# Moving the turn of the expert rows by one chunk, and other VectorE work between a chunk's inputs and its weights

## Chip, cores and metric

The kernel runs on one core of one Trainium2 chip. The metric is the device time of one execution in microseconds (us). The time of the kernel before is the median of three runs.

## What is computed

Four sequences of 1024 tokens with 128 features pass through four blocks, each followed by a residual sum and a layer norm: a state-space mixer with a gated MLP (L0 attention), a mixture of 8 linear experts with the best 2 per token (L0 ffn), an attention of 16 heads with relative positions (L1 attention), and a second mixture of 8 gated experts with a capacity of 512 rows (L1 ffn).

```python
x = _layernorm(x + _L0_attn_ref(x, ...))   # mixer, then MLP
x = _layernorm(x + _L0_ffn_ref(x, ...))    # 8 experts, best 2
x = _layernorm(x + _L1_attn_ref(x, ...))
x = _layernorm(x + _L1_ffn_ref(x, ...))
```

In the first expert layer each token's logits give a softmax, the two largest shares are kept, and the output is the sum of the two experts' products weighted by these shares.

## The kernel before, in words

Every engine has its own written-out program; engines meet at semaphores only, and each engine takes its instructions in order. The first phase, up to about 560 us, runs the first two blocks and the projections of the attention. Then comes the attention (560 to about 1270 us), then the second expert layer.

The first phase is a pipeline over the four sequences, written as a table of slots:

```python
SLOTS = [(0, None, None), (1, 0, None), (2, 1, 0), (3, 2, 1), (None, 3, 2), (None, None, 3)]
SCALED_AT = {3: (0,), 4: (1, 2), 5: (3,), 6: (4, 5), 7: (6,)}
BIAS_AT, LAST_PAIR = 5, 7
```

In a slot (m, p, q), sequence m is in the mixer, p in the MLP and the first expert layer, q in the projections to queries, keys and values. Slots are counted from 0 here, so slots 1, 2 and 3 hold a mixer and an expert layer together, slots 2, 3 and 4 an expert layer and projections.

The second half of a slot is a loop of eight turns c = 0 to 7, one for each chunk of 128 tokens of the mixer's scan; the parts of p and q are spread over the same turns. For the mixer, turn c has these steps:

- **TensorE**: `chunk_carried` (the carried state's output), `chunk_state` (the new state), then for chunk c + 1 `chunk_front` (three transposes and one product) and `chunk_after` (sums of decays), then `chunk_out` (the output of chunk c).
- **ScalarE**: `chunk_copy` (line 1347, which waits for VectorE's `Gm`) and `chunk_exp` (line 1353, the decays L) of chunk c + 1, then `decays_so_far` (line 1364, four copies) of chunk c + 2.
- **GpSimd**: `chunk_decays`, two products of 128x256: `xw` (line 1613), which needs VectorE's inputs, and `hdec` (line 1617), which `chunk_carry` of the next turn needs.
- **VectorE**: `chunk_carry` (line 1973, needs the new state from TensorE and `hdec`), `chunk_scaled` (1990), then for chunk c + 1 `chunk_inputs` (1964, and 1967, which writes `Gm`) and `chunk_weights` (1979, needs `Gm` and ScalarE's L).

Into the same turns go the steps of the expert layer of p: VectorE's `normalise` (line 1866, eight instructions, in turn 0) writes the rows `x2`; TensorE's `rows_turned_moe` transposes them; ScalarE's `evac_T("moe", ...)` (1238) copies the result to `xnT`; TensorE's `route0` forms the routing logits; VectorE's `route_logits` and `route_shift` (1878 to 1885) take them in turn 1, ScalarE's `route_exp` and VectorE's `route_shares` (from 1889) follow in turn 2, and `route_which` to `gate_parts` in turn 3. TensorE's `expert_pair` k = 0 to 7 multiplies two tiles of rows with four experts; VectorE's `experts_scaled(p, k)` (2084) adds the products with their shares, 8 instructions for each k, by the table `SCALED_AT`. In turn 5 `bias_added` (2065) follows.

For q, queries and keys are cut into three bf16 parts: ScalarE's `cut_part` (1322, 1324, in turns 0, 1 and 2) writes a part, and VectorE's `cut_rest` (2129, 2133, in turns 0 and 1) subtracts it. `cut_part` s = 1 and 2 need the remainder of s - 1.

## Time and profile before

| what | us |
|---|---|
| median of 3 runs (1388.61 to 1392.61) | 1392.61 |
| the profiled execution, its own time | 1390.74 |
| its span, first to last instruction | 1389.0 |
| VectorE busy in the span | 1090.6 (79%) |
| TensorE matmuls busy in the span | 1239.2 (89%) |

All views read one execution. Times in them are from the start of the span. A bracket at a row's end says how long the engine was idle before it and what released it. Instructions of an engine overlap a little, so a start can lie before the end of the row ahead.

The slots lie about so: slot 1 from 112 to 190 us, slot 2 to 312, slot 3 to 438, slot 4 to 526, slot 5 to 560.

### The profile page before, as it was taken

The numbers are of one execution on the slowest core, as the hardware profiler recorded it, in microseconds if no ns is written. First come the engines' busy times: TensorE is split into PE (matmuls) and PEld (weight loads), VectorE is DVE, ScalarE is ACT, GpSimd is POOL, SyncE is SP. The second block draws the span as 40 slices with busy tenths as digits, with TensorE's granted clock in tenths as the row PEclk, the third lists the DMA queues.
The fourth block names the chain that finished last, engine by engine and source line by source line (L and its number), as shares of the span: only waits on it lengthen the run. The fifth ranks groups of instructions, "written<-read, shape, count | busy, mean of one in ns | idle before, by whom it ended". The sixth has DMA issues, their size and how long they took to land. (4 is left out here: it accounts for less than half of the span.)

```text
span 1389.0 us, 39431 instructions
## 1 busy us (share of the span) xinstructions
PE 1239.2 (89%) x16528; PEld 647.8 (47%) x16528; DVE 1090.6 (79%) x2184; ACT 902.1 (65%) x1739; POOL 285.0 (21%) x417
## 2 busy tenths in 40 slices
PE   5998888788887877999999999999999999994895
PEld 2556445453644522454555444444444544432462
DVE  6787787789676688899999989999999998944123
ACT  5665345437432302899998888888889988893242
POOL 2222131121112104200000110511104211034472
PEclk9999999999989988999999999999999999997998
DMA  5080000200113812111102211122102200011135
GB/s 141 1 230 16 1 2 16 108 2 1 61 49 74 152 68 109 44 38 44 43 17 62 52 45 35 46 68 54 43 18 56 62 22 18 18 34 46 45 108 188
DMA packets 59703, 77.72 MB, mean 56 GB/s; under 512 B 15010, under 2 KB 41189, under 8 KB 57686
## 3 DMA queue, kind: packets, MB, share of 16 engines
q1 hardware_dynamic: 56454, 70.95, 19.2%
q0 software_dynamic: 3072, 4.25, 1.0%
q8 instruction: 131, 2.15, 0.7%
q14 instruction: 46, 0.38, 0.1%
HBM read 37.18 MB, written 40.03 MB: 56 GB/s over the span
## 5 line engine op out<-in xcount | busy, mean ns | idle before, releaser
L1479 ACT ACTIVATE space<-ps 128x512 f32<-128x512 f32 x1024 | 605.2, 598 | 86.4 <-PE ps L667 37.2
L2139 DVE TENSOR_REDUCE smax<-ps 128x1 f32<-128x1024 f32 x512 | 613.3, 1220 | 51.1 <-PE ps L667 26.4
L667 PE MATMUL ps<-space 96*32 96x512 bf16 (+2 forms) x8432 | 609.9, 381 | 24.8 <-DVE smax L2139 13.8
L667 PEld LDWEIGHTS ps<-space 96*32 96x32 bf16 (+2 forms) x8432 | 251.4, 98 | 292.1 <-DVE smax L2139 44.2
L1047 PE MATMUL ps<-space 128*9 128x256 f32 x4096 | 315.8, 379 | 0.0
L1047 PEld LDWEIGHTS ps<-space 128*9 128x9 f32 x4096 | 116.2, 92 | 100.1 <-ACT space L1479 0.4
L1347 ACT ACTIVATE btok<-ps 128x128 f32<-128x128 f32 x32 | 8.9, 277 | 125.5 <-issue 101.5
L667 PE MATMUL ps<-w_exp,xnT 128*128 128x512 f32 x128 | 72.4, 694 | 14.4 <-DVE x L2084 14.4
L2084 DVE SCALAR_TENSOR_TENSOR x<-ps,gsel,x 128x128 f32<-128x128 f32 x256 | 69.1, 342 | 12.4 <-PE ps L667 12.1
L667 PE MATMUL ps<-ones,ident 128*128 128x512 bf16 x228 | 58.8, 418 | 17.4 <-POOLq L1695 12.3
L1949 DVE SCALAR_TENSOR_TENSOR space<-space,conv_w 128x512 f32<-128x512 f32 x96 | 71.2, 750 | 2.3
L1584 POOL TENSOR_SCALAR eps_sum<-mv 128x4 f32<-128x4 f32 x32 | 7.4, 231 | 318.3 <-DVEq L1855 317.6
L1691 POOL DMA_INDIRECT expert_in<-space,slot x64 | 63.0, 984 | 34.9 <-issue 19.3
L667 PE MATMUL ps<-space,w_in 128*128 128x512 f32 x96 | 58.6, 719 | 8.2 <-DVE x L2019 3.3
L1675 POOL TENSOR_TENSOR xnT<-x,xa 128x512 f32<-128x512 f32 x6 | 7.7, 1282 | 233.4 <-DMA xa<-den_rows 233.4
L1613 POOL TENSOR_TENSOR space<-space,decay 128x256 f32<-128x256 f32 x28 | 17.1, 612 | 155.6 <-issue 109.8
L667 PEld LDWEIGHTS ps<-ones,ident 128*128 128x128 bf16 x228 | 23.6, 106 | 50.4 <-issue 18.2
L1979 DVE TENSOR_TENSOR space<-space,Gm 128x512 f32<-128x512 f32 x32 | 24.6, 769 | 27.2 <-ACT space L1353 27.2
L667 PEld LDWEIGHTS ps<-w_exp,xnT 128*128 128x128 f32 x128 | 25.3, 215 | 44.0 <-issue 23.7
L1586 POOL TENSOR_TENSOR rstd<-eps_sum,neg_half 128x4 f32<-128x4 f32 x40 | 41.6, 1039 | 3.3
L1364 ACT ACTIVATE aU<-upto,av 128x128 f32<-128x128 f32 x128 | 40.6, 395 | 0.0
L667 PE MATMUL ps<-xnT,w_gate 128*128 128x512 f32 x64 | 34.9, 628 | 5.6 <-DVE space L2038 4.8
(250 smaller groups left out, 1375.4 us busy)
## 6 DMA issues: line engine op xcount, KB each, us to landing
head_sums<-space SPq DMA_DIRECT2D x31, 256.0 KB, 2.3
q_rows<-space SPq DMA_DIRECT2D x24, 256.0 KB, 2.4
k_rows<-space SPq DMA_DIRECT2D x24, 256.0 KB, 2.8
space<-k_rows SPq DMA_DIRECT2D x16, 384.0 KB, 5.4
space<-q_rows SPq DMA_DIRECT2D x16, 384.0 KB, 7.1
expert_out<-x_all SPq DMA_DIRECT2D x2, 2048.0 KB, 18.5
space<-expert_out SPq DMA_DIRECT2D x4, 1024.0 KB, 9.5
v_rows<-space SPq DMA_DIRECT2D x4, 576.0 KB, 3.3
```

Of the source, the lines that this page charges most:

```text
L667: return nc.tensor.matmul(out, lhsT, rhs, start=first, stop=last)
L1047: last = nc.tensor.matmul(bank(run_bank(N))[COLS * g:COLS * g + VSTEP, q0:q0 + PV_COLS], v_now[:, b % 2, kt, lo:lo + VSTEP], prob[:, QUAD ...
L1347: nc.scalar.activation(btok[:, c % 2], bank(TRB)[:, 2 * P:3 * P], ACT.Copy).then_inc(S.btok_ready, 1)
L1364: last = nc.scalar.activation(aU[:, c % 2, h], upto[:], ACT.Copy, scale=av[:, c, h:h + 1])
L1479: nc.scalar.activation(prob[:, QUAD * (step % PROB_SETS) + unit % QUAD, :], bank(STB + unit % 2), ACT.Exp)\
L1586: g.tensor_tensor(out, eps_sum[:, 0:n], neg_half[:, 0:n], ALU.pow).then_inc(done, 1)
L1613: g.tensor_tensor(xw[:, c % 2], xdt[:, c % 2], decay[:, 0, c].unsqueeze(2).to_broadcast([P, SSM_HEADS, SSM_DIM]), ALU.mult).then_inc(S.xw_ ...
L1691: g.indirect_dma_start(expert_in, bass.IndirectOffsetOnAxis(ap=slot[:, k, i:i + 1], axis=0), xrow[:, i, k, :], None, bounds_check=E * CAPA ...
L1949: ins = v.scalar_tensor_tensor(out, raw[:, f, lo + k:lo + k + HALF], conv_w[:, f, k:k + 1], out, ALU.mult, ALU.add)
L1979: v.tensor_tensor(Wm[:, c % 2], EL[:, c % 2], Gm[:, c % 2].unsqueeze(1).to_broadcast([P, SSM_HEADS, P]), ALU.mult).then_inc(S.w_ready, 1)
L2084: ins = v.scalar_tensor_tensor(x2[:, i, :], tiles4(EXPERT_BANKS[k][w])[:, e, :], gsel[:, i, HT * (k % 2) + e:HT * (k % 2) + e + 1], x2[:, ...
L2139: v.tensor_reduce(smax[:, N % 2, i:i + 1], ps[:, b0:b0 + 2, :].rearrange("p k n -> p (k n)"), AX.X, ALU.max).then_inc(S.s_max, 1)
```

## The change

Nothing is computed differently, only the order of instructions on TensorE, ScalarE and VectorE changes; GpSimd's and SyncE's programs stay.

- `rows_turned_moe` moves from the end of turn 0 to turn 1, after `chunk_after` and ahead of `chunk_out`; `evac_T("moe", ...)` moves to turn 1 too, behind that turn's copy, exponential and decays, and so behind `cut_part` of turn 0.
- On VectorE `normalise` moves ahead of `chunk_weights` in turn 0.
- `cut_rest` s = 0 and 1 move from the end of turns 0 and 1 to turns 1 and 2, ahead of `chunk_weights`.
- In turns 4 and 6 the first of the two `experts_scaled` (k = 1 and k = 4) moves ahead of `chunk_weights`.

```diff
--- before.py
+++ after.py
@@ -960,6 +960,8 @@
                             chunk_state(m, c)
                             chunk_front(m, c + 1)
                             chunk_after(m, c + 1)
+                    if p is not None and c == 1:
+                        rows_turned_moe(p)
                     if p is not None and c == BIAS_AT:
                         gates_turned(p)
                     if p is not None and c in PRODUCTS_AHEAD:
@@ -973,8 +975,6 @@
                         if c == NT - 1:
                             mix_out(m, 0)
                     if p is not None:
-                        if c == 0:
-                            rows_turned_moe(p)
                         if c == 1:
                             route0(p)
                         if c == 2 and m is None:
@@ -1426,7 +1426,7 @@
                         evac_gates(p)
                     if m is not None and c in (2, 4, 6):
                         gated_squares(m, c // 2 - 1)
-                    if p is not None and c == 0:
+                    if p is not None and c == 1:
                         evac_T("moe", p, (7, 5))
                     if p is not None and c == 2:
                         route_exp(p)
@@ -2191,6 +2191,19 @@
                         chunk_carry(m, c)
                         chunk_scaled(m, c)
                         chunk_inputs(m, c + 1)
+                    if p is not None and c == 0:
+                        for H in range(2):
+                            normalise(xa, x2, H, 0, 6 * p + H)
+                    if q is not None and p is not None and c in (1, 2):
+                        cut_rest(q, c - 1)
+                    if m is not None and p is not None and HT <= c < NT - 1:
+                        ahead = SCALED_AT[c][:1]
+                    else:
+                        ahead = ()
+                    for k in ahead:
+                        if c != BIAS_AT:
+                            experts_scaled(p, k)
+                    if m is not None and c < NT - 1:
                         chunk_weights(m, c + 1)
                     if m is not None and c == NT - 1:
                         chunk_scaled(m, c)
@@ -2201,9 +2214,6 @@
                         if m + 1 < B:
                             input_norm(m + 1)
                     if p is not None:
-                        if c == 0:
-                            for H in range(2):
-                                normalise(xa, x2, H, 0, 6 * p + H)
                         if c == 1:
                             route_logits(p, 6, b_route0)
                             route_shift(p)
@@ -2216,15 +2226,14 @@
                             gate_parts(p)
                     if p is not None:
                         for k in SCALED_AT.get(c, ()):
-                            experts_scaled(p, k)
+                            if k not in ahead or c == BIAS_AT:
+                                experts_scaled(p, k)
                             if c == BIAS_AT:
                                 bias_added(p)
                                 expert_statistics(p, 0)
                             if m is None and k in MAXIMA_IN_SUMS:
                                 for pair in MAXIMA_IN_SUMS[k]:
                                     pair_max(pair)
-                    if q is not None and p is not None and c < 2:
-                        cut_rest(q, c)
                     if m is not None and c % 2 == 1 and c < NT - 1:
                         gate(m, c // 2)
                 if m is not None:
```

VectorE, slot 2, turns 0 and 1, in the kernel before (1973 carry, 1990 scaled, 1964 and 1967 inputs, 1979 weights, 1866 normalise, 2129 and 2133 remainders):

```order
L1964 TENSOR_TENSOR space<-ps,dt 128x256
L1967 TENSOR_TENSOR Gm<-ps,upto 128x128
L1979 TENSOR_TENSOR space<-space,Gm 128x512
L1866 TENSOR_SCALAR x<-xa,mv,rstd 128x128 x8
L2129 TENSOR_TENSOR space<-space 128x1024
L2133 TENSOR_TENSOR space<-space 128x1024
L1973 TENSOR_TENSOR hst<-hdec,ps 128x256
L1990 TENSOR_TENSOR space<-ps,decay 128x256
L1964 TENSOR_TENSOR space<-ps,dt 128x256
L1967 TENSOR_TENSOR Gm<-ps,upto 128x128
```

and with the change:

```order
L1964 TENSOR_TENSOR space<-ps,dt 128x256
L1967 TENSOR_TENSOR Gm<-ps,upto 128x128
L1866 TENSOR_SCALAR x<-xa,mv,rstd 128x128 x8
L1979 TENSOR_TENSOR space<-space,Gm 128x512
L1973 TENSOR_TENSOR hst<-hdec,ps 128x256
L1990 TENSOR_TENSOR space<-ps,decay 128x256
L1964 TENSOR_TENSOR space<-ps,dt 128x256
L1967 TENSOR_TENSOR Gm<-ps,upto 128x128
L2129 TENSOR_TENSOR space<-space 128x1024
L2133 TENSOR_TENSOR space<-space 128x1024
L1979 TENSOR_TENSOR space<-space,Gm 128x512
```

Each of the two weights now has other work between it and its inputs, and the remainders stand one turn later, behind the second inputs.

ScalarE, slot 2, turns 0 and 1 (1238 copies the turned rows to `xnT`, 1322 and 1324 cut queries and keys, 1347 to 1364 are the copy, the exponential and the decays):

```order
-L1238 ACTIVATE xnT<-ps 128x512 x2
-L1322 ACTIVATE space<-space 128x1024
-L1324 ACTIVATE space<-space 128x1024
-L1347 ACTIVATE btok<-ps 128x128
-L1353 ACTIVATE space<-ps 128x512
-L1364 ACTIVATE aU<-upto,av 128x128 x4
+L1322 ACTIVATE space<-space 128x1024
+L1324 ACTIVATE space<-space 128x1024
+L1347 ACTIVATE btok<-ps 128x128
+L1353 ACTIVATE space<-ps 128x512
+L1364 ACTIVATE aU<-upto,av 128x128 x4
+L1238 ACTIVATE xnT<-ps 128x512 x2
```

The copy of the turned rows went from ahead of the first cut to behind the next chunk's decays.

VectorE, slot 2, turn 4 (2084 adds the scaled expert products):

```order
 L1964 TENSOR_TENSOR space<-ps,dt 128x256
 L1967 TENSOR_TENSOR Gm<-ps,upto 128x128
-L1979 TENSOR_TENSOR space<-space,Gm 128x512
-L2084 SCALAR_TENSOR_TENSOR x<-ps,gsel,x 128x128 x16
+L2084 SCALAR_TENSOR_TENSOR x<-ps,gsel,x 128x128 x8
+L1979 TENSOR_TENSOR space<-space,Gm 128x512
+L2084 SCALAR_TENSOR_TENSOR x<-ps,gsel,x 128x128 x8
 L1973 TENSOR_TENSOR hst<-hdec,ps 128x256
```

Eight of the sixteen instructions went ahead of the weights.

## Rows read from the trace of the kernel before

**Rows 1.** Busy time by engine, slot 2 (us: PE, PEld, DVE, ACT, POOL; clock, DMA, GB/s)

```profile
190.00:312.00 122.00, 102.07 (x742) 60.51 (x746) 96.37 (x292) 59.25 (x144) 23.71 (x37) 0.93 0.10 36
```

**Rows 2.** Waits of VectorE from 120 to 440 us: total us, times, longest us

```profile
DVE space L1979 <- ACT space L1353: 20.2, 22, 1.7
...
DVE space L2129 <- ACT space L1322: 6.2, 4, 2.6
...
DVE red L1889 <- ACT sc L1334: 3.1, 3, 1.0
```

**Rows 3.** Timeline of VectorE, slot 2: start us, us, instructions, [idle before <-releaser]

```profile
245.68 0.80 DVE L1979 TENSOR_TENSOR space<-space,Gm 128x512 f32<-128x512 f32 x1 [0.88 <-ACT space L1353]
246.40 2.13 DVE L1866 TENSOR_SCALAR x<-xa,mv,rstd 128x128 f32<-128x128 f32 x8
251.15 1.23 DVE L2129 TENSOR_TENSOR space<-space 128x1024 f32<-128x1024 f32 x1 [2.62 <-ACT space L1322]
...
254.42 0.28 DVE L1967 TENSOR_TENSOR Gm<-ps,upto 128x128 f32<-128x128 f32 x1
...
268.01 0.42 DVE L1973 TENSOR_TENSOR hst<-hdec,ps 128x256 f32<-128x256 f32 x1 [1.16 <-PE ps L667]
```

**Rows 4.** Timeline of ScalarE, slot 2

```profile
249.57 0.60 ACT L1238 ACTIVATE xnT<-ps 128x512 f32<-128x512 f32 x1 [0.65 <-PE ps L654]
...
255.43 1.27 ACT L1364 ACTIVATE aU<-upto,av 128x128 f32<-128x128 f32 x4
```

**Rows 5.** Timeline of TensorE, slot 2: the routing products

```profile
255.55 0.72 PE L667 MATMUL ps<-w_route,xnT 128*32 128x8 f32 x64
```

**Rows 6.** Timeline of VectorE, slot 1

```profile
125.74 0.69 DVE L1979 TENSOR_TENSOR space<-space,Gm 128x512 f32<-128x512 f32 x1 [1.69 <-ACT space L1353]
...
130.17 0.42 DVE L1973 TENSOR_TENSOR hst<-hdec,ps 128x256 f32<-128x256 f32 x1 [1.68 <-PE ps L667]
...
133.41 0.23 DVE L1878 TENSOR_TENSOR lg<-ps,b_route 128x64 f32<-128x64 f32 x1 [0.29 <-PE ps L667]
```

**Rows 7.** Timeline of TensorE, slot 1: last products of loop turn 0

```profile
126.02 0.71 PE L769 MATMUL ps<-ident,space 128*128 128x128 f32 x4
```

**Rows 8.** Timeline of VectorE, slot 3

```profile
390.20 0.42 DVE L1973 TENSOR_TENSOR hst<-hdec,ps 128x256 f32<-128x256 f32 x1 [1.22 <-PE ps L667]
```

**Rows 9.** Timeline of VectorE, slot 4

```profile
481.61 1.22 DVE L2129 TENSOR_TENSOR space<-space 128x1024 f32<-128x1024 f32 x1 [2.32 <-ACT space L1322]
...
498.36 2.16 DVE L2084 SCALAR_TENSOR_TENSOR x<-ps,gsel,x 128x128 f32<-128x128 f32 x8 [1.14 <-PE ps L667]
```

**Rows 10.** Timeline of TensorE, slot 4

```profile
494.07 0.62 PE L667 MATMUL ps<-space 96*32 96x512 bf16 x8 [2.51 <-DVE smax L2139]
```

**Rows 11.** Timeline of VectorE, slot 2, loop turn 4

```profile
279.11 0.78 DVE L1979 TENSOR_TENSOR space<-space,Gm 128x512 f32<-128x512 f32 x1 [0.88 <-ACT space L1353]
```

**Rows 12.** Timeline of VectorE, slot 1: weights beside GpSimd

```profile
121.35 0.91 DVE L1979 TENSOR_TENSOR space<-space,Gm 128x512 f32<-128x512 f32 x1 [0.88 <-ACT space L1353]
```

**Rows 13.** Timeline of GpSimd, slot 1: its carry product at that place

```profile
121.67 1.06 POOL L1617 TENSOR_TENSOR hdec<-hst,decay 128x256 f32<-128x256 f32 x1
```

**Rows 14.** All weights and all carry products: duration ns min/median/max, first and last start

```profile
L1979 DVE TENSOR_TENSOR space<-space,Gm x32: 681/785/910, 43.0 to 420.3; 128x512 f32<-128x512 f32 x32
...
L1617 POOL TENSOR_TENSOR hdec<-hst,decay x28: 612/612/1062, 42.6 to 408.1; 128x256 f32<-128x256 f32 x28
```

**Rows 15.** Busy time and granted clock of a short stretch (columns as in Rows 1)

```profile
157.00:161.00 4.00, 3.76 (x6) 1.22 (x6) 2.16 (x6) 2.54 (x11) 1.18 (x2) 0.50 0.00 0
```

**Rows 16.** Timeline of TensorE, slot 1, loop turn 5: one expert pair

```profile
157.24 3.78 PE L667 MATMUL ps<-w_exp,xnT 128*128 128x512 f32 x4 [1.83 <-DVE x L2084]
```

**Rows 17.** Timeline of TensorE, slot 2, loop turn 4: one expert pair

```profile
275.59 1.98 PE L667 MATMUL ps<-w_exp,xnT 128*128 128x512 f32 x4 [1.08 <-DVE x L2084]
```

**Rows 18.** Timeline of VectorE, slot 1, loop turn 5

```profile
161.13 2.16 DVE L2084 SCALAR_TENSOR_TENSOR x<-ps,gsel,x 128x128 f32<-128x128 f32 x8 [1.09 <-PE ps L667]
164.53 1.48 DVE L2065 TENSOR_TENSOR x<-x,ps 128x512 f32<-128x512 f32 x2 [1.24 <-PE ps L667]
```

## The prediction

> **What bounds the kernel now.** I read the busy times by stretch first, then the list of waits, then the timelines of the slots that the change touches. In slot 2 VectorE is busy 96.37 of 122 us and TensorE's matmuls, whose spans overlap, 102.07 [rows 1]: neither is full, so it is waits that matter, and which of them lie on a chain. VectorE's list has three that the change aims at: 20.2 us in 22 waits of the weights for ScalarE's exponential, 6.2 us in 4 waits of the remainders for ScalarE's cut, 3.1 us in 3 waits of the routing shares [rows 2]. They are on the path that ends last, because the others mostly wait for VectorE's last result, as the brackets on TensorE show (a maximum, a scaled sum) [rows 10, 16, 17]. So a wait that VectorE loses moves everything behind it, up to the next point where VectorE waits for something that does not move. The attention behind the first phase starts when the last slot's work is done, and keeps its length.
>
> The regular wait is 0.88 us [rows 3, 11]: VectorE has written `Gm`, ScalarE then copies and exponentiates, and only then can the weights run. Work put there, as long as it is over 0.88 us and ready, removes it. Nothing is added or removed; the same instructions run.
>
> **Slot 2.** In turns 0, 1 and 2 the fillers are 2.13 us of normalise [rows 3] and twice two remainders of 1.23 us [rows 3]; each is over 0.88, so 3 x 0.88 = 2.64 goes. The remainders waited 2.62 [rows 3] and, in the next turn, about 0.6 (the four waits of slots 2 and 3 sum to 6.2 [rows 2]; with 2.62 here, and 2.32 for the long one of slot 3 as in slot 4 [rows 9], 1.2 is left for the two short ones): ScalarE's first cut stood behind the copy of the turned rows, which stood behind normalise, transposes and all. Now the cut runs while VectorE normalises, and is there before it is asked for: 3.2 goes. The shares waited 1.03, a third of 3.1 [rows 2], so the exponential they need ends 0.88 + 0.79 + 1.03 = 2.7 us behind `Gm`, and now 2.3 of remainders and 0.7 of weights lie between: it goes. The carry of turn 3 waited 1.16 for TensorE [rows 3]; TensorE's expert pair ahead of it starts when `chunk_scaled` is done, and 2.3 us more of VectorE's work now lies between that and the carry: it goes. Sum removed: 2.64 + 3.2 + 1.03 + 1.16 = 8.0.
>
> What is late next is the turned rows. Call T the end of the second `Gm` (254.42 + 0.28 in the old order). ScalarE's decays end 2.0 us behind it, at 256.70 [rows 4]; now the two copies of 0.60 [rows 4] follow, overlapping a little, to T + 3.1, and the routing product of 0.72 [rows 5] to T + 3.8. VectorE has the remainders and weights, 2.3 + 0.7, ready at T + 3.0, so `route_logits` waits 0.8 that it did not wait before. Behind it in order stand the gate and the next carry. Net of turns 0 to 2: 8.0 - 0.8 = 7.2.
>
> In turns 4 and 6 the filler is eight scaled sums, 2.16 us [rows 9], whose products TensorE forms a turn earlier (turn 4) or in the same turn ahead of the chunk's output (turn 6; if they come late, at worst the 0.88 comes back). 2 x 0.88 = 1.8 [rows 11].
>
> **A new cost: GpSimd beside VectorE.** GpSimd starts its two products of 0.61 us as soon as the inputs are written, so they ran in the gap that is now filled. Where one met VectorE's weights, both stretched: the weights took 0.91 [rows 12] and the carry product 1.06 [rows 13], against minima of 0.68 and 0.61 [rows 14]; usually the weights take 0.79, the tail of a GpSimd product costing 0.1. The scaled sums read PSUM and one tensor of SBUF; no row shows them beside GpSimd, and I take none for them. For a filler of turns 0 to 2 the bounds are 0 (0.1 less than now, as the weights no longer meet GpSimd) and 1.22 (both products ahead of VectorE); I take 0.45, the stretch of 1.06 - 0.61, as the nearest row. In slots 2 and 3 it counts in turns 0 and 2, since in turn 1 the 0.8 wait takes it up: 0.9 for each.
>
> The Trainium skill (SBUF — State Buffer, SBUF: two separate sides) has a rule against this change: VectorE and GpSimd share one pair of ports, and whichever of a VectorE instruction with two SBUF inputs or in a two-port mode and a GpSimd instruction that reads SBUF starts first holds it for its whole length. The stretched pair [rows 12, 13] agrees. By that rule GpSimd, which starts first, would hold each filler back for up to both products, and the sum would be that of the second rival below.
>
> Slot 2: 7.2 + 1.8 - 0.9 = 8.1.
>
> **Slot 3** is the same, with 1.22 [rows 8] for the carry's 1.16: the remainders lose 3.0 (6.2 less 3.2), so 2.64 + 3.0 + 1.03 + 1.22 = 7.9 goes, 0.8 comes, + 1.8 - 0.9: 8.0.
>
> **Slot 1** has no q, so no remainders. `Gm` of turn 0 ended at 125.74 - 1.69 = 124.05 [rows 6]. Normalise and weights now end at 124.05 + 2.13 + 0.69 = 126.9. The carry waited until 130.17 [rows 6], because TensorE put the transposes ahead of the state product. Without them TensorE is free at 126.7 [rows 7] and has two products of 256 columns to do, at most 1.0 by half of an expert pair [rows 17]: carry at 127.8 (bounds 126.9 and 130.17), 2.4 earlier. T, four instructions of 0.3 to 0.4 later, is 129.05. But with no remainders VectorE is idle from weights to T + 3.8 = 132.85, against 133.41 before [rows 6]: of 2.4 only 0.5 is kept, the rest turns into a wait of about 2.2 at `route_logits`. With 1.8 from turns 4 and 6: 2.3. GpSimd's stretch disappears in the wait for the state.
>
> **Slot 4** has no mixer; only ScalarE's order changes. The remainders' wait of 2.32 [rows 9] goes but for 0.1: 2.2. TensorE's idle 2.51 in front of a score pair [rows 10] shrinks by as much, and the wait of 1.14 for the next expert pair [rows 9], which then ran slow, goes: 3.3 (bounds 0 and 5.6, the latter if a later pair gains the 2.33 that rows 18 show).
>
> **Sum**: 2.3 + 8.1 + 8.0 + 3.3 = 21.7. From the profiled execution's own 1390.74: **1369.0**. That execution lies 1.9 under the median of the runs shown, 1392.61, so the same gain from the median would be 1370.9.
>
> **Rivals.**
>
> *TensorE keeps its clock.* In turn 5 of slots 1 and 3 an expert pair takes 3.78 [rows 16] at a granted clock of 0.50, the 1.2 GHz level [rows 15], against 1.98 in slot 2 [rows 17], behind 1.83 us of idle; VectorE then waits 1.09 + 1.24 = 2.33 [rows 18]. With eight sums done ahead of the weights, what TensorE waits for there comes earlier, and its idle time is shorter. If both stay fast: 2 x 2.33 more, 1364.3. Against: no row shows which idle time decides. Chance 0.13.
>
> *GpSimd holds VectorE for both products.* 1.22 instead of 0.45 in turns 0 and 2, and 0.4 over the 0.8 in turn 1, in slots 2 and 3: 2 x (2 x 0.77 + 0.4) = 3.9, 1372.9. For it: GpSimd is first by the timeline, and its results are not late. Against: the only rows show 0.1 to 0.45. Chance 0.16.
>
> *The routing chain is longer.* If TensorE runs turn 1 at the low level, the outputs and routing products ahead of `route_logits` double, up to 2 more in slots 1 to 3: about 1375. The change shortens TensorE's idle time there, which speaks against it. Chance 0.07.
>
> *Slower.* The place is TensorE's clock over the loops: every expert pair at the low level costs VectorE what turn 5 shows, 2.33. The 32 pairs of slots 1 to 4 would have to hold 11 slow ones more than now to eat 21.7 and 4.2 besides (26 / 2.33); with 12, 1369.0 + 28 = 1397. It would take longer idle stretches on TensorE, and the change shortens them. Chance 0.02.
>
> *Nothing moves*, because something that VectorE does not drive, such as the loads for the attention, sets the end of the first phase: 1391. The profile shows no such wait. Chance 0.03.
>
> **How the numbers follow.** The forecast has 0.59, with the rivals 0.13, 0.16, 0.07, 0.02 and 0.03. The range takes in the first two rivals (1364 to 1373) with some 2 to 4 us on each side for slot 4's bounds and for the spread of runs, 1388.61 to 1392.61: **1361 to 1377**. About 0.3%, 4.2 us, is what a measurement of this kernel can tell: faster 0.95, same 0.03, slower 0.02.
>
> **What would show it.** In the new profile the weights' waits for the exponential should fall from 22 to about 9 between the same slots (turns 3 and 5 of three slots, turns 1 and 2 of slot 1, little else); the remainders should not wait; `route_logits` should wait about 2.2 in slot 1 and up to 0.8 in slots 2 and 3; the shares and the carry of turn 3 should not wait in slots 2 and 3. GpSimd's products or the fillers should be longer by some tenths. The attention should begin about 22 us earlier and last as long. It would be wrong if `route_logits` waited over 3 us, or if the expert pairs at the low clock became more.

## The result, and the profile after

| | before | after |
|---|---|---|
| median of the timed runs, us | 1390.61 (4 runs) | 1365.79 (4 runs, 1364.55 to 1367.16) |
| the profiled execution's span, us | 1389.0 | 1362.8 |
| VectorE busy in the span, us | 1090.6 | 1091.7 |
| TensorE's matmuls busy in the span, us | 1239.2 | 1225.2 |
| GpSimd busy in the span, us | 285.0 | 295.2 |
| start of the attention in the profile, us | 559.67 | 533.55 |

The ratio of the times is 0.9833, with a 95% interval of 0.9811 to 0.9855: 20.2 to 26.3 us faster, 24.8 between the medians. The forecast was 1369.0, a gain of 21.7. VectorE does the same work in the same busy time; waits went. GpSimd is busy 10 us more: its products were held up beside VectorE's work, as will be seen.

Slot 2, in the columns of [rows 1]: it is 8.1 us shorter with VectorE busy for the same time.

```profile
184.30:298.20 113.90, 99.18 (x748) 59.38 (x752) 96.82 (x291) 59.06 (x144) 28.59 (x37) 0.94 0.11 39
```

VectorE's waits in the new profile from 118 to 425 us, the same slots as in [rows 2] (columns: total us, times, longest us).

```profile
DVE space L1979 <- ACT space L1353: 7.9, 9, 0.9
...
DVE lg L1878 <- PE ps L667: 4.5, 3, 2.1
...
DVE red L1889 <- ACT sc L1334: 1.0, 1, 1.0
```

The weights wait 9 times instead of 22, as forecast; the remainders (L2129) no longer stand in the list; the shares (L1889) wait in one slot only. New is the wait of the logits (L1878), 2.14 us in slot 1, 1.28 and 1.11 in slots 2 and 3.

VectorE's timeline of the new profile, slot 2, turns 0 to 2, against [rows 3].

```profile
238.98 2.84 DVE L1866 TENSOR_SCALAR x<-xa,mv,rstd 128x128 f32<-128x128 f32 x8
...
243.34 0.28 DVE L1967 TENSOR_TENSOR Gm<-ps,upto 128x128 f32<-128x128 f32 x1
243.54 1.21 DVE L2129 TENSOR_TENSOR space<-space 128x1024 f32<-128x1024 f32 x1
...
245.81 0.68 DVE L1979 TENSOR_TENSOR space<-space,Gm 128x512 f32<-128x512 f32 x1
247.77 0.23 DVE L1878 TENSOR_TENSOR lg<-ps,b_route 128x64 f32<-128x64 f32 x1 [1.28 <-PE ps L667]
...
251.17 1.22 DVE L2129 TENSOR_TENSOR space<-space 128x1024 f32<-128x1024 f32 x1
252.30 1.63 DVE L2133 TENSOR_TENSOR space<-space 128x1024 f32<-128x1024 f32 x1
253.86 1.10 DVE L1979 TENSOR_TENSOR space<-space,Gm 128x512 f32<-128x512 f32 x1
...
256.29 0.42 DVE L1973 TENSOR_TENSOR hst<-hdec,ps 128x256 f32<-128x256 f32 x1
```

The carry of turn 3 (the last row) has no bracket. Between its second `Gm` and that carry the kernel before took 268.01 - 244.52 = 23.5 us, the change 256.29 - 238.79 = 17.5: 6.0 less, against 7.2 - 0.9 = 6.3 forecast.

GpSimd's timeline of the new profile, slot 2, turns 0 to 2: L1613 is the product for the state, L1617 the one for the carry.

```profile
239.01 0.61 POOL L1613 TENSOR_TENSOR space<-space,decay 128x256 f32<-128x256 f32 x1 [6.96 <-DVE space L1964]
239.59 0.62 POOL L1617 TENSOR_TENSOR hdec<-hst,decay 128x256 f32<-128x256 f32 x1
243.55 3.41 POOL L1613 TENSOR_TENSOR space<-space,decay 128x256 f32<-128x256 f32 x1 [3.35 <-issue]
...
251.19 1.67 POOL L1613 TENSOR_TENSOR space<-space,decay 128x256 f32<-128x256 f32 x1 [3.65 <-issue]
252.82 1.59 POOL L1617 TENSOR_TENSOR hdec<-hst,decay 128x256 f32<-128x256 f32 x1
```

Three places, three outcomes, though by the trace VectorE's work starts first in each, by 0.01 to 0.03 us. In turn 0 GpSimd is undisturbed and normalise takes 2.84 instead of 2.13: 0.71 lost. The loss lies in the first two of its eight instructions, which end 0.08 us behind GpSimd's second product; shown alone they are this row of VectorE's timeline:

```profile
238.98 1.30 DVE L1866 TENSOR_SCALAR x<-xa,mv,rstd 128x128 f32<-128x128 f32 x2
```

In turn 1 VectorE is undisturbed and GpSimd's product takes 3.41 instead of 0.61. In turn 2 both pay: second remainder 1.63 for 1.22, weights 1.10 for 0.68, so 0.83 lost. There the engines take turns, one whole instruction each: first remainder, product, second remainder, product and weights end at 252.39, 252.86, 253.93, 254.41 and 254.96. In turn 4 the scaled sums and GpSimd's products run side by side, and neither is longer than alone (VectorE's timeline, then GpSimd's):

```profile
266.43 2.15 DVE L2084 SCALAR_TENSOR_TENSOR x<-ps,gsel,x 128x128 f32<-128x128 f32 x8
```

```profile
266.45 0.61 POOL L1613 TENSOR_TENSOR space<-space,decay 128x256 f32<-128x256 f32 x1 [7.76 <-issue]
```

TensorE's timeline of the new profile, slot 2, turn 1; then the busy times and the granted clock (0.50) of the two us from the routing products on, in the columns of [rows 1]; then ScalarE's copies of the turned rows. After the transposes (L654) and the output of the chunk TensorE is idle 1.96 us until ScalarE has copied, and then the routing products and those of the state run slow.

```profile
242.43 1.04 PE L654 MATMUL ps<-ident,x 128*128 128x128 f32 x8
...
246.65 1.04 PE L667 MATMUL ps<-w_route,xnT 128*32 128x8 f32 x64 [1.96 <-ACT xnT L1238]
247.63 1.22 PE L667 MATMUL ps<-hst,space 128*128 128x256 f32 x2
```

```profile
246.60:248.60 2.00, 1.95 (x66) 1.79 (x67) 0.77 (x4) 1.89 (x3) 0.93 (x2) 0.50 0.34 122
```

```profile
245.52 1.08 ACT L1238 ACTIVATE xnT<-ps 128x512 f32<-128x512 f32 x2
```

TensorE's expert pair of turn 5, slot 1, in the new profile, and VectorE's sums and bias that waited for it in [rows 18]: the pair takes 1.99 us, not the 3.78 of [rows 16], and both waits are gone.

```profile
154.93 1.99 PE L667 MATMUL ps<-w_exp,xnT 128*128 128x512 f32 x4 [1.49 <-DVE x L2084]
```

```profile
157.65 2.15 DVE L2084 SCALAR_TENSOR_TENSOR x<-ps,gsel,x 128x128 f32<-128x128 f32 x8
159.84 1.28 DVE L2065 TENSOR_TENSOR x<-x,ps 128x512 f32<-128x512 f32 x2
```

The time from profile to profile, slot by slot, in us. A slot is read here from VectorE's second `Gm` in it to the start of the last four sums of the mixer's residual (line 2019 of the kernel before); "1 to 2" and "2 to 3" are the stretches between; "slot 4" runs from the end of slot 3 to the start of the attention on TensorE. The last column is the ratio of the timed runs to those of the kernel before, with its interval. The experiments follow below.

| profile | slot 1 | 1 to 2 | slot 2 | 2 to 3 | slot 3 | slot 4 | attention starts | ratio |
|---|---|---|---|---|---|---|---|---|
| before | 66.49 | 54.26 | 69.49 | 52.94 | 71.19 | 121.53 | 559.67 | 1 |
| before, again | 66.48 | 53.89 | 68.17 | 52.96 | 69.74 | 120.02 | 554.83 | 1.0016 [0.9997, 1.0034] |
| the change | 60.87 | 54.27 | 61.38 | 54.32 | 60.89 | 118.17 | 533.55 | 0.9833 [0.9811, 0.9855] |
| the change, again | 61.30 | 52.89 | 61.33 | 54.34 | 60.80 | 118.59 | 533.53 | 0.9836 [0.9815, 0.9857] |
| scalings only | 61.56 | 52.88 | 67.32 | 54.28 | 65.50 | 121.28 | 546.67 | 0.9932 [0.9911, 0.9954] |
| no scalings | 63.13 | 52.89 | 63.16 | 52.94 | 62.52 | 115.77 | 535.29 | 0.9873 [0.9849, 0.9898] |
| fast clock | 63.67 | 54.25 | 69.27 | 54.32 | 70.03 | 119.06 | 554.90 | 0.9967 [0.9955, 0.9979] |
| no turn | 60.09 | 52.88 | 62.00 | 54.33 | 61.48 | 117.71 | 532.74 | 0.9848 [0.9826, 0.9870] |
| slot 4 old | 60.93 | 53.41 | 61.03 | 52.96 | 60.87 | 121.74 | 535.16 | 0.9837 [0.9810, 0.9864] |
| small products | 59.80 | 52.88 | 59.33 | 52.95 | 58.68 | 117.42 | 524.13 | 0.9769 [0.9743, 0.9795] |
| gate first | 60.13 | 52.89 | 61.19 | 54.32 | 60.83 | 118.26 | 532.22 | 0.9809 [0.9782, 0.9836] |
| searches first | 60.15 | 52.89 | 60.22 | 52.94 | 59.85 | 118.68 | 528.92 | 0.9789 [0.9766, 0.9813] |
| copies first | 60.83 | 52.88 | 60.01 | 52.95 | 59.46 | 115.75 | 525.71 | 0.9802 [0.9780, 0.9823] |
| copies and searches first | 58.16 | 52.89 | 58.95 | 54.32 | 58.34 | 116.78 | 523.08 | 0.9776 [0.9755, 0.9797] |

What lies behind the start of the attention takes 828.1 to 832.9 us in these profiles, with no order that follows the edits, so the columns of the slots tell more than the span.

### The profile page after: what moved, and what is told of

The parts are those of the page before. It is cut to its first block and busy times, and to the rows that moved or that the text cites. A ratio compares the mean times of both kernels' runs of the same rounds, so it can differ in the third digit from the quotient of the medians.

```text
span 1362.8 us, 39431 instructions
## 1 busy us (share of the span) xinstructions
PE 1225.2 (90%) x16528; PEld 644.6 (47%) x16528; DVE 1091.7 (80%) x2184; ACT 901.7 (66%) x1739; POOL 295.2 (22%) x417
## 5 line engine op out<-in xcount | busy, mean ns | idle before, releaser
L667 PE MATMUL ps<-w_exp,xnT 128*128 128x512 f32 x128 | 66.4, 643 | 12.8 <-DVE x L2084 12.8
L1613 POOL TENSOR_TENSOR space<-space,decay 128x256 f32<-128x256 f32 x28 | 24.9, 889 | 129.6 <-issue 83.7
```

Of the source, the lines that this page charges most:

```text
L667: return nc.tensor.matmul(out, lhsT, rhs, start=first, stop=last)
L1613: g.tensor_tensor(xw[:, c % 2], xdt[:, c % 2], decay[:, 0, c].unsqueeze(2).to_broadcast([P, SSM_HEADS, SSM_DIM]), ALU.mult).then_inc(S.xw_ ...
```

## The experiments

**How much is chance.** The change and the kernel before were each run and profiled once more.

> The change once more, unaltered, to tell what of the differences between the experiments belongs to the kernel and what to the execution. Where TensorE fell to the low level in the profile of the change (the hidden layer's products in the first halves of slots 2 and 3, 1.4 us each against other experiments) it falls again if the program's own timing decides it: the stretches between the slots are 54.3 and 54.3 us again, and the attention starts within 1 us of 533.55. If chance in the execution decides, these stretches differ by 1.4 from one profile to the next.

> The kernel before once more, unaltered. If its own timing makes TensorE fall to the low level in turn 5 of slots 1 and 3, as in its first profile, the expert pair takes 3.78 us there again (from the sixth to the seventh Gm of the slot 11.8 us instead of 9.3), in slot 2 1.98. If it was chance in that one execution, at least one of the two is fast now or slot 2 is slow, and the 4.8 us that the change gained there are not the change's.

The start of the attention repeats within 0.02 us for the change, but only because differences cancel: the stretch "1 to 2" is 52.89 instead of 54.27, while slot 1 is 0.4 longer and began 0.6 later. "2 to 3" repeats at 54.34. In "1 to 2" TensorE's products for the MLP's hidden layer were slow in the first profile of the change (granted clock 0.57 from 215.6 to 217.4 us) and not in the second (1.00 from 216.6 to 217.8), behind a little less idle time (TensorE's timeline, first the change, then the change again):

```profile
215.60 1.88 PE L667 MATMUL ps<-xnT,w_gate 128*128 128x512 f32 x2 [2.04 <-DVE space L2038]
```

```profile
216.67 1.12 PE L667 MATMUL ps<-xnT,w_gate 128*128 128x512 f32 x2 [1.71 <-DVE space L2038]
```

So a piece of 1.4 us can come or go from one execution to the next. The kernel before, profiled again, starts its attention 4.8 us earlier than the first time, in pieces of 1.3 to 1.5 in slots 2, 3 and 4. The slow pairs of turn 5 are there again in slots 1 and 3, a little shorter, and in slot 2 not:

```profile
158.01 3.30 PE L667 MATMUL ps<-w_exp,xnT 128*128 128x512 f32 x4 [1.83 <-DVE x L2084]
...
404.55 3.54 PE L667 MATMUL ps<-w_exp,xnT 128*128 128x512 f32 x4 [1.83 <-DVE x L2084]
```

From the seventh to the eighth `Gm` of the slot (number 6 and 7, counted from 0; turn 5 lies between) it takes 10.6 and 10.5 us there, 11.8 in both slots the first time, 9.3 in slot 2, where the pair is fast: these waits belong to the kernel, their length varies.

Slot 2's piece of 1.3 is, but for 0.2, the wait of 1.16 of the carry of turn 3 [rows 3], which the prediction counted among the waits that the order of the instructions makes. TensorE's expert pair ahead of that carry took 2.63 us in the first profile of the kernel before and 1.88 in the second, and there the carry doesn't wait (TensorE's timelines, first and second profile):

```profile
264.38 2.63 PE L667 MATMUL ps<-w_exp,xnT 128*128 128x512 f32 x4
```

```profile
262.73 1.88 PE L667 MATMUL ps<-w_exp,xnT 128*128 128x512 f32 x4
```

The granted clock was 0.64 in the first (262.3 to 267.0 us), 1.00 in the second (261.6 to 264.7). Over slots 2 and 3 of the four profiles that keep VectorE's old order in turns 0 to 3 (the kernel before twice, "scalings only" and "fast clock") the carry waits 1.16 to 1.24 in the six where this pair ran slow and not in the two where it ran fast. So this wait was the clock's, too.

**The sums ahead of the weights, and TensorE's clock in turn 5.** First the sums alone, in the kernel before:

```diff
+                        if p is not None and c in (4, 6):
+                            experts_scaled(p, SCALED_AT[c][0])
                         chunk_weights(m, c + 1)
...
```

> The kernel before with one part of the change alone: in turns 4 and 6 of slots 1 to 3 eight of the scaled sums stand ahead of the weights. Both theories give a gain of 1.19 (turn 4) and 0.92 (turn 6) per slot, as the change showed: 3 x 2.1 = 6.3 us. Theory A: the sums done earlier also shorten TensorE's idle time ahead of turn 5's expert pair and so keep its clock in slots 1 and 3; then that pair takes 1.98 instead of 3.78 us, the waits of 1.09 + 1.24 for it go, and the gain is 6.3 + 2 x 2.4 = 11.1 us, a ratio to the kernel before of 0.992. Theory B: the clock in turn 5 came from what the change moved in turns 0 to 3; then the pair stays at 3.78 in slots 1 and 3, the gain is 6.3, the ratio 0.9955.

Then the change without them:

```diff
-                    if m is not None and p is not None and HT <= c < NT - 1:
-                        ahead = SCALED_AT[c][:1]
-                    else:
-                        ahead = ()
+                    ahead = ()
```

> The change without the sums ahead of the weights in turns 4 and 6; the rest of it stays. Theory A (the sums ahead keep TensorE's clock in turn 5): the pair of turn 5 in slots 1 and 3 takes 3.78 again and VectorE waits 1.09 + 1.24 for it, so 11.1 of the 26 us gained are lost, ratio about 0.991. Theory B (what was moved in turns 0 to 3 keeps it): the pair stays at 1.98, 6.3 are lost, ratio about 0.988.

The pair of turn 5 in slot 1, with the sums alone and with the rest alone (TensorE's timelines):

```profile
155.62 1.99 PE L667 MATMUL ps<-w_exp,xnT 128*128 128x512 f32 x4 [1.49 <-DVE x L2084]
```

```profile
157.33 1.98 PE L667 MATMUL ps<-w_exp,xnT 128*128 128x512 f32 x4 [1.83 <-DVE x L2084]
```

Alone, the sums shorten slots 1 to 3 by 4.9, 2.2 and 5.7 us, in slots 1 and 3 with a fast pair: theory A's 11.1 and some more, of which 1.2 lies between the fourth and fifth `Gm` of slot 3, where the edit does nothing (the carry's wait above, which did not occur there this time). Taking them out of the change costs 2.3, 1.8 and 1.6 in the slots, 5.7 in all, and the pairs stay fast: theory B's figure. So either half of the change is enough to free turn 5 of the low clock, and theory A's second prediction fell. The idle time right ahead of the pair does not decide it: it is 1.83 where the pair is slow [rows 16] and 1.83 in the row above. Whether it takes part was asked by filling it, in the kernel before:

```diff
                     if p is not None and c == BIAS_AT:
                         gates_turned(p)
+                        if m is not None:
+                            keep_clock(4, 6)
```

> The kernel before, and on TensorE six products of the identity with ones, written to a bank that nobody reads, between the turned gates and the expert pair of turn 5 in slots 1 to 3: they fill part of its 1.83 us of idle time there and change nothing else. If that idle time lowers the clock, the pairs of slots 1 and 3 take 1.98 instead of 3.78 and VectorE's waits of 1.09 + 1.24 go in both: 4.7 us less, ratio 0.9966; the idle time left is about 0.5. If the clock falls for another reason, the pairs stay at 3.78, the six products themselves run longer, and the time is the same or up to 1 us longer per slot.

TensorE's timeline, slot 1, turn 5, of that kernel:

```profile
155.45 1.46 PE L667 MATMUL ps<-ones,ident 128*128 128x512 bf16 x6
157.44 1.98 PE L667 MATMUL ps<-w_exp,xnT 128*128 128x512 f32 x4 [0.53 <-DVE x L2086]
```

The pair is fast in both slots, turn 5 takes 9.26 us in both, and the timed runs gain 0.0033 [0.0021, 0.0045], 4.6 us, against 4.7 expected. By the timed runs the low clock in turn 5 cost 2.9 to 6.2 us, which fits the waits of the first profile; this profile alone would not show it, since its attention starts where that of the kernel before, again, does (554.90 and 554.83). What else, ahead of that idle time, has to come together is open.

**The turn of the rows.** TensorE and ScalarE at their old places, VectorE as in the change:

```diff
-                    if p is not None and c == 1:
-                        rows_turned_moe(p)
...
+                        if c == 0:
+                            rows_turned_moe(p)
...
-                    if p is not None and c == 1:
+                    if p is not None and c == (1 if m is None else 0):
                         evac_T("moe", p, (7, 5))
```

> The change with the turn of the rows put back to turn 0 on TensorE and on ScalarE in slots 1 to 3 (slot 4 keeps the new order); VectorE's order is that of the change. Theory 1, the prediction's: the turn one chunk later is worth little by itself, since what it takes from the carry comes back as the wait of the routing logits (2.1 us in slot 1, 1.1 to 1.3 in slots 2 and 3). Then the wait of the logits vanishes, the carry of turn 1 waits 1 to 3 us for TensorE instead, and the time is within 2 us of the change: ratio 0.982 to 0.985. Theory 2: the turn's place is a main term; then the carry's wait (up to 3 us in slot 1) and late cuts on ScalarE (the remainders wait about 1 us again) come on top, 5 us or more slower than the change, ratio 0.987 or higher.

VectorE's timeline, slot 2: the carry of turn 1, and the logits behind the weights.

```profile
241.93 0.42 DVE L1973 TENSOR_TENSOR hst<-hdec,ps 128x256 f32<-128x256 f32 x1 [1.08 <-PE ps L667]
...
246.84 0.21 DVE L1878 TENSOR_TENSOR lg<-ps,b_route 128x64 f32<-128x64 f32 x1
```

The slots are 0.8 shorter, 0.6 longer and 0.6 longer than in the change: 0.4 in sum, and the ratio is 0.9848, at the end of theory 1's range. Theory 1 holds: one wait (1.1 us for the state) is traded for another (1.3 for the logits). In slots 1 to 3 the gain is VectorE's order; the turn on TensorE and ScalarE is worth next to nothing there. One thing more is traded: with the old place GpSimd's product of turn 1 is not starved, it gets in behind the first remainder as in turn 2, and the second remainder pays, in slots 2 and 3 alike (slot 2, turn 1, VectorE's and GpSimd's timelines):

```profile
244.26 1.64 DVE L2133 TENSOR_TENSOR space<-space 128x1024 f32<-128x1024 f32 x1
```

```profile
243.15 1.67 POOL L1613 TENSOR_TENSOR space<-space,decay 128x256 f32<-128x256 f32 x1 [4.52 <-issue]
```

**Slot 4.** ScalarE's old order there alone:

```diff
-                    if p is not None and c == 1:
+                    if p is not None and c == (0 if m is None else 1):
                         evac_T("moe", p, (7, 5))
```

> The change with ScalarE's old order in slot 4 alone: there the turned rows are copied ahead of the first cut again. The prediction's term for slot 4 says that the attention starts 3.3 us later behind the start of slot 4 than in the change (the first remainder waits 2.3 us again, and the expert pair 1.1), ratio to the kernel before 0.9857 instead of 0.9833. The rival, that slot 4's gain came from the phase at which the slot is reached: the attention starts within 1 us of the change.

VectorE's timeline, slot 4, with the old order:

```profile
457.02 1.23 DVE L2129 TENSOR_TENSOR space<-space 128x1024 f32<-128x1024 f32 x1 [2.32 <-ACT space L1322]
...
473.82 2.16 DVE L2084 SCALAR_TENSOR_TENSOR x<-ps,gsel,x 128x128 f32<-128x128 f32 x8 [1.19 <-PE ps L667]
```

Both waits of [rows 9] are back, and slot 4 takes 121.74 instead of 118.17 and 118.59: 3.2 to 3.6 longer, as the prediction's term has it. Over all profiles of the table slot 4 takes 119.1 to 121.7, mean 120.7, in the five with the old order, 115.8 to 118.7, mean 117.5, in the nine with the new. The ratio does not show it: 0.9837 against the change's 0.9833 where 0.9857 was expected, and its interval holds all three. In the profile the two stretches between the slots were 2.2 shorter that time, so the attention starts only 1.6 later.

**GpSimd beside VectorE.** Its two products cut to one column in 64 (this kernel leaves out most of the carried state in slots 1 to 3):

```diff
-                g.tensor_tensor(xw[:, c % 2], xdt[:, c % 2],
+                n = SSM_DIM if b == 0 else 1
+                g.tensor_tensor(xw[:, c % 2, :, 0:n], xdt[:, c % 2, :, 0:n],
...
-                g.tensor_tensor(hdec[:], hst[:, c % 2],
+                g.tensor_tensor(hdec[:, :, 0:n], hst[:, c % 2, :, 0:n],
...
```

> The change with GpSimd's two products of a chunk cut to one column of 64 per head in slots 1 to 3 (the carried state is then not what the reference has, so the routing and what hangs on it differ; the start of the attention is what is read). If GpSimd's reads stretch VectorE's fillers: normalise of turn 0 takes 2.13 instead of 2.84, the second remainder of turn 2 1.22 instead of 1.63, the weights behind it 0.69 instead of 1.10, and the attention starts 2 x 1.5 + 0.7 = 3.7 us earlier than in the change at most, 2 at least (part is taken up by waits for the turned rows). If they are long for another reason (ScalarE, their own data), their durations stay and the start moves by less than 1 us.

VectorE's normalise (turn 0) and second remainder (turn 2) of that kernel, slot 2, then GpSimd's products of turns 0 and 1:

```profile
235.95 2.14 DVE L1867 TENSOR_SCALAR x<-xa,mv,rstd 128x128 f32<-128x128 f32 x8
...
248.23 1.22 DVE L2134 TENSOR_TENSOR space<-space 128x1024 f32<-128x1024 f32 x1
```

```profile
235.98 0.20 POOL L1614 TENSOR_TENSOR space<-space,decay 128x4 f32<-128x4 f32 x1 [7.80 <-DVE space L1965]
...
239.82 2.99 POOL L1614 TENSOR_TENSOR space<-space,decay 128x4 f32<-128x4 f32 x1 [3.47 <-issue]
```

VectorE's durations are back, so the stretch came from GpSimd's products. The slots are 1.1, 2.1 and 2.2 us shorter, 5.3 in sum where 3.7 was expected at most: the logits waited 0.94 for 1.28, too, and the weights took 0.69 for 0.78 in the turns that still wait. (The other 4.1 of the earlier attention lie between the slots, in slot 4 and ahead of slot 1, in pieces that vary between other profiles too.) The last row is the clearest reading of the study: a product of four columns, 0.20 us of work, takes 2.99, and ends at 242.81, as VectorE's two remainders and the weights behind them end (242.75).

The Trainium skill (SBUF — State Buffer, SBUF: two separate sides) calls the pair of ports shared by the two engines an exclusive lock, not a split of bandwidth. The traces agree that one side stands still while the other runs: GpSimd in turn 1, each in its turn in turn 2, the first two instructions of normalise in turn 0. In two points they don't bear out what the prediction drew from the rule. By the starts in the trace VectorE comes first in all three turns, and yet normalise is the side that waits in turn 0; and it lost 0.71, not 1.22.

**Three further steps.** The gate ahead of the logits in turn 1:

```diff
                         if c == 1:
+                            if m is not None:
+                                gate(m, 0)
                             route_logits(p, 6, b_route0)
...
```

> The change, and in turn 1 of slots 1 to 3 the gate of the first two chunks (three instructions, 1.5 us) stands on VectorE ahead of the routing logits instead of behind them. It needs only the outputs of chunks 0 and 1, which TensorE has some 0.7 us before the routing product. If the wait of the logits (2.1, 1.3, 1.1 us) is on the path, 0.7 to 1.5 of it goes in each slot: the attention starts about 3 us earlier than in the change, ratio to the kernel before 0.981. If the wait hid something else (ScalarE's exponential for the shares, TensorE's next chunk), it comes back behind and the start moves by less than 1 us.

VectorE's timeline, slot 2: the logits no longer wait, the carry behind them does.

```profile
246.83 0.21 DVE L1878 TENSOR_TENSOR lg<-ps,b_route 128x64 f32<-128x64 f32 x1
...
248.62 0.42 DVE L1973 TENSOR_TENSOR hst<-hdec,ps 128x256 f32<-128x256 f32 x1 [1.07 <-PE ps L667]
```

Slots 2 and 3 gain 0.2 and 0.1, slot 1 0.7, and the attention starts 1.3 earlier, not 3. The ratio, 0.9809, is the expected 0.981, but its interval holds the change's 0.9833, and the slots don't show the gain. A miss, near to what the rival said: TensorE forms the routing products ahead of the state, so what delays the one delays the other. What delays both is ScalarE's copy. It was put ahead of the next chunk's copy and exponential:

```diff
+                    if p is not None and m is not None and c == 1:
+                        evac_T("moe", p, (7, 5))
                     if m is not None and c < NT - 1:
                         chunk_copy(m, c + 1)
                         chunk_exp(m, c + 1)
...
-                    if p is not None and c == 1:
+                    if p is not None and m is None and c == 1:
                         evac_T("moe", p, (7, 5))
```

> The change with one step of ScalarE put earlier: in turn 1 of slots 1 to 3 it copies the turned rows ahead of the next chunk's copy and exponential instead of behind the chunk's decays. Theory: what delays the routing product, the logits, and behind them on TensorE the state product of the next carry is ScalarE's place for the copies (they wait for nothing else: the transposes end before the second Gm of the turn). Then the routing product starts about 2 us earlier, at full clock since TensorE's idle 1.96 us ahead of it is gone, the logits wait for under 0.3 us in slots 2 and 3, and the next carry comes 1.3 us earlier in slots 2 and 3 and 1.7 in slot 1 (there the weights start 0.5 later): the attention starts 4.4 us earlier. Rival: GpSimd's product for the state, starved beside the remainders until 246.9, holds the next carry where it is in slots 2 and 3; then the carry waits for it, and only slot 1's 1.7 is gained.

TensorE's timeline, slot 2, turn 1:

```profile
243.38 0.72 PE L667 MATMUL ps<-w_route,xnT 128*32 128x8 f32 x64
...
245.77 0.70 PE L667 MATMUL ps<-space,btok 128*128 128x256 f32 x2 [1.03 <-POOL space L1615]
```

The logits wait for nothing, and the next `Gm`, number 3, stands 1.36 and 1.32 us closer behind number 1 in slots 2 and 3, as expected. TensorE now waits for GpSimd's starved product, but ends in time for the carry. In slot 1 it was 0.5 where 1.7 was expected, and as much is lost again at the slot's end, in VectorE's waits for TensorE. With no remainders ahead of them, VectorE's weights wait for the exponential that now stands behind the copy (VectorE's timeline, slot 1):

```profile
131.34 0.69 DVE L1981 TENSOR_TENSOR space<-space,Gm 128x512 f32<-128x512 f32 x1 [2.33 <-ACT space L1353]
```

Most of these 2.33 us are not the order's. TensorE ran turn 0 of this slot at a granted clock of 0.58 (123.0 to 126.7 us) and turned the rows at 128.87; in the run with both steps, below, the same products ran at 1.00, the rows were turned at 127.09, and the weights waited 1.09 (TensorE's timelines, this run and that one):

```profile
123.09 1.92 PE L667 MATMUL ps<-aU,after 128*128 128x512 f32 x2
```

```profile
122.72 1.02 PE L667 MATMUL ps<-aU,after 128*128 128x512 f32 x2
```

The attention starts 7.8 us earlier, but only 2.8 of it in slots 1 to 3; slot 4 (2.4) and the stretches between (2.8) are nothing that the edit touches. The third step is the searches of the routing ahead of the weights in turn 3:

```diff
+                    if m is not None and p is not None and c == HT - 1:
+                        route_which(range(NT))
                     for k in ahead:
...
                         if c == HT - 1:
-                            route_which(range(NT))
+                            if m is None:
+                                route_which(range(NT))
```

> The change, and in turn 3 of slots 1 to 3 the eight index searches of the routing (1.15 us) stand on VectorE between the chunk's inputs and its weights, where it still waits 0.9 us for the exponential. By the mechanism that the prediction used, the three waits go, less what GpSimd's two products cost beside the searches: 1.5 to 2.6 us, ratio to the kernel before about 0.982. If VectorE is not what bounds turn 3, the time saved turns up as a wait at the next carry, and the start of the attention moves by less than 0.5 us.

VectorE's weights and GpSimd's products beside the searches, slot 2, turn 3:

```profile
257.07 0.69 DVE L1979 TENSOR_TENSOR space<-space,Gm 128x512 f32<-128x512 f32 x1
```

```profile
255.88 0.61 POOL L1613 TENSOR_TENSOR space<-space,decay 128x256 f32<-128x256 f32 x1 [3.11 <-issue]
256.45 0.61 POOL L1617 TENSOR_TENSOR hdec<-hst,decay 128x256 f32<-128x256 f32 x1
```

The wait is gone, neither engine is stretched, and from `Gm` number 4 to number 5 each slot is 1.06 us shorter, 0.88 of it the wait and 0.1 the weights, which no longer meet GpSimd. Slots 1 to 3 together gain 2.9, a little more than the 2.6 expected.

> The step of evac_first and that of which_first together (the index searches of turn 3 ahead of the weights). If the two are on different stretches of one chain they add: 2.9 us within the slots as in which_first and what evac_first gives, 4.4 by its theory: the attention starts about 7 us earlier than in the change, ratio to the kernel before about 0.978. If the second only moves a wait of the first, the sum is under 4.

Together the two take 2.7, 2.4 and 2.6 us from slots 1 to 3, 7.7 in sum, against 2.9 and 2.8 alone: they add, and what is over lies in slot 1, where 2.1 is gained by `Gm` number 3 this time, for 0.5 above at the low clock. The attention starts 10.5 earlier than in the change. The time is 1357.83 us, the ratio 0.9776 [0.9755, 0.9797]: the fastest version here that computes all of it.

## Why the prediction was right

- **The path.** VectorE's waits were on it, and what they gave up arrived at the attention. Slot by slot, the first profiles gained 5.6 (forecast 2.3), 8.1 (8.1), 10.3 (8.0), 3.4 (3.3), less 1.4 between slots 2 and 3: 26.1 at the start of the attention. Against the second profile of the kernel before it is 21.3, and 23.2 by the ratio.
- **The fills.** Turn 4 gave 1.2 and turn 6 0.7 to 0.9 per slot against 0.88 each. In turn 4, 0.1 of the excess is the weights, which no longer meet GpSimd; most of the rest is the 0.08 us by which an instruction without a wait starts ahead of the end of the one before (243.54 against 243.34 + 0.28 in the rows above). The remainders and the shares lost their waits as worked out.
- **The carry of turn 3.** It lost its wait too, but its reason was misread: the 1.16 and 1.22 were the expert pair's at a low clock, and in slot 2 of the second profile of the kernel before there was no such wait to lose.
- **"`route_logits` waits 0.8 that it did not wait before."** It waited 1.28 and 1.11 in slots 2 and 3: TensorE, idle 1.96 us ahead of them, formed the routing products in slot 2 at a granted clock of 0.50, the 1.2 GHz level, in 1.04 instead of 0.72. This is the third rival's mechanism, in small. The prediction argued that TensorE's idle time shrinks there; ahead of these products it grew, from none [rows 5]. Nor is the wait all new: in slot 2 of the kernel before, again, the products took 1.04 too, and the logits waited 0.77. Slot 1's 2.2 came as 2.14.
- **"I take 0.45" for GpSimd's stretch.** Mis-sized: 0.71 in turn 0, 0.83 in turn 2, nothing in turn 1: 1.5 per slot for 0.9. And GpSimd, not only VectorE, was held back: 3.41 us. "GpSimd, which starts first" did not hold: the fillers start 0.01 to 0.03 us ahead of its product.
- **The first rival happened beside the forecast**: the pairs of turn 5 in slots 1 and 3 are fast, 2.6 us in each by the first profile of the kernel before, 1.2 to 1.3 by the second. Its figure, 1364.3, lies nearer to the measured 1365.8 than the forecast's 1369.0 does, and its chance of 0.13 was too low. Its reason, the shorter idle time behind the sums, is enough but not needed: without the sums that time is 1.83 again, and the clock stays.
- **Slot 4** came as worked out, and taking the step back returns it.
- **The other rivals** did not occur: the second's 1.22 per place is not reached, `route_logits` waited under 3 us, and no more expert pairs became slow.

Costs were set 1.2 (GpSimd, 2 x 0.6) and 0.8 (logits) too low, gains 2.5 to 5.1 (the clock of two pairs) and 0.9 (the fills, 2.1 per slot instead of 1.8) too low; that makes 23.1 to 25.7 of 21.7, about the 20.2 to 26.3 that the timed runs give. So the mechanism, VectorE's waits on the chain, was right, but that the sum came so near is in part luck. Slot 2's 8.1 for 8.1 is such a case: 1.1 more of costs was made up by 0.3 more from the fills and by about 0.8 that the prediction did not have, the shorter weights of turns 0 and 1 and the 0.08 us that goes with each wait.

## What to carry to other kernels

Where an engine writes an operand, and waits for another engine to answer, put ready work of at least the answer's length between; it pays even when the list of waits shows only 0.9 us each, if they lie on the chain. Choose that work by what it reads: beside GpSimd's products, index searches and sums out of PSUM cost nothing, a normalise or a subtraction of SBUF tensors costs 0.7 to 0.8 us or starves GpSimd. And when a wait of one step has been removed by moving another, look in the other engines' order (here ScalarE's) for what is now late, before reordering the waiting engine again.

## What the runs showed of the hardware

- A GpSimd product of four columns, 0.20 us of work, took 2.99 us beside three VectorE instructions that follow each other without a gap, two subtractions of 1.22 and the weights; in turn 2, beside the same instructions, one of full size got in after the first subtraction (1.67 us) and stretched the next two. The outcome repeats from execution to execution, and it isn't the VectorE instructions alone that decide: with the rows turned in turn 0 again, turn 1 went as turn 2 does (1.67). What decides is open.
- TensorE fell to the low level behind 1.83 us of idle time in some slots and not in others, the same ones in both profiles of the kernel before; the slow pairs took 3.78 us in one execution, 3.30 and 3.54 in the next. At other places pieces of 1.2 to 1.5 us came and went between executions of one kernel; in the two shown above the granted clock differed (0.57 and 1.00, 0.64 and 1.00). So one profile against another can be 5 us off without any edit.
